# A graph network of four layers: scores of a batch as one product and one sum, and the next-block step moved from behind the passes to their heads

## The reference, cut to what matters

```python
# second layer
Q = node_feats[src] @ W_q + b_q
K = node_feats[dest] @ W_k + b_k
bias = edge_feats @ W_e + b_e
pre = Q + K + bias
act = jnp.where(pre >= 0, pre, SLOPE * pre)
scores = act @ a_w + a_b
...
# last layer
q = x[dst] @ Wq_w + Wq_bias
key_base = x_src @ Wk1 + rel_emb @ Wk2 + Wk_bias
score_base = jnp.einsum('eo,eo->e', q, key_base)
```

## Time and profile before

| what | value |
|---|---|
| median of 3 runs | 8316.85 us (8298.67 to 8347.98) |
| the profiled execution | 8297.37 us, its span 8295.3 us |
| granted TensorE clock over the span | 0.738 |
| busy over the span | PE 63%, DVE 56%, ACT 50%, POOL 60% |

### The profile page before, as it was taken

How to read it: one execution, slowest core, us unless ns; L and a number is a source line. 1 busy time by engine, 2 the same in 40 slices (tenths; PEclk the granted TensorE clock), 3 DMA queues, 4 the chain that set the end, 5 groups by cost and what they waited for, 6 DMA issues and landing times. The chain is left out here.

```text
span 8295.3 us, 160086 instructions
## 1 busy us (share of the span) xinstructions
PE 5185.0 (63%) x37998; PEld 3831.1 (46%) x38194; DVE 4646.3 (56%) x21263; ACT 4171.3 (50%) x11643; POOL 4948.9 (60%) x5713
## 2 busy tenths in 40 slices
PE   4666666666664444445445449996666666666664
PEld 3556555655552222222222228884444444444443
DVE  5555555555545454455445459996555555555556
ACT  3555555555524343344344349993555555555554
POOL 5555555555536556556556539993566666666663
PEclk7888888888876666666666669997666666666666
DMA  3333333333334444455444438884222222222221
GB/s 113 90 89 88 90 88 90 88 90 89 89 91 135 132 134 132 133 134 138 132 132 135 129 99 269 268 267 175 64 63 64 64 64 64 64 63 65 63 64 42
DMA packets 673100, 908.82 MB, mean 110 GB/s; under 512 B 141463, under 2 KB 430217, under 8 KB 672730
## 3 DMA queue, kind: packets, MB, share of 16 engines
q1 hardware_dynamic: 502654, 605.53, 23.3%
q0 software_dynamic: 168944, 301.30, 15.1%
q10 hardware_dynamic: 1357, 0.47, 0.0%
HBM read 696.57 MB, written 210.28 MB: 109 GB/s over the span
## 5 line engine op out<-in xcount | busy, mean ns | idle before, releaser
L801 POOL DMA_INDIRECT rows<-src_rows,idx_slots x1531 | 1469.1, 960 | 1007.9 <-issue 485.3
L801 POOL DMA_INDIRECT rows<-rel_rows,idx_slots x1531 | 1451.3, 948 | 967.3 <-remote 397.0
L801 POOL DMA_INDIRECT rows<-node_rows,idx_slots x1339 | 1279.3, 955 | 928.6 <-remote 338.6
L1399 ACT ACTIVATE onehot<-ident,fresh_slots 128x128 f32<-128x128 f32 x3136 | 993.0, 387 | 1501.5 <-remote 1079.1
L1390 PE MATMUL bank<-onehot,ones 128*128 128x512 f32 x1568 | 1317.0, 937 | 215.5 <-issue 129.8
L1097 ACT ACTIVATE dst_pairs<-pre,minus_node 128x512 bf16<-128x512 int16 x816 | 581.1, 718 | 1091.9 <-remote 589.5
L1488 PE MATMUL bank<-w_e,edge_in 128*128 128x256 f32 x784 | 405.8, 616 | 1045.7 <-remote 504.9
L1127 PE MATMUL bank<-by_chunk,dst_pairs 128*128 128x192 bf16 x6144 | 775.9, 270 | 301.8 <-issue 232.8
L1488 PEld LDWEIGHTS bank<-w_e,edge_in 128*128 128x128 f32 x784 | 210.5, 300 | 1438.3 <-issue 1103.9
L1127 PEld LDWEIGHTS bank<-by_chunk,dst_pairs 128*128 128x128 bf16 x6144 | 585.4, 108 | 381.0 <-issue 281.8
L1127 PE MATMUL bank<-wide_room,dst_pairs 128*128 128x192 bf16 x3264 | 477.6, 278 | 452.1 <-ACT dst_pairs L1101 255.6
(11 more groups left out here) (309 smaller groups left out, 11923.4 us busy)
## 6 DMA issues: line engine op xcount, KB each, us to landing
edge_in<-dst_line SPq DMA_DIRECT2D x392, 256.0 KB
spill<-rows SPq DMA_DIRECT2D x392, 256.0 KB
rows<-spill SPq DMA_DIRECT2D x392, 256.0 KB, 3.1
hot_rows<-rows SPq DMA_DIRECT2D x98, 712.0 KB
onehots<-hot_rows SPq DMA_DIRECT2D x196, 356.0 KB, 3.5
onehots<-src_low SPq DMA_DIRECT2D x98, 512.0 KB
edge_in<-in_ea_l SPq DMA_DIRECT2D x98, 256.0 KB
edge_in<-in_eaT_l SPq DMA_DIRECT2D x392, 64.0 KB
```

The source lines that it names most:

```text
L801: pool.indirect_dma_start(out=to[:, b.slot(ROW_RING), g, :], out_offset=None, in_=table, in_offset=bass.IndirectOffsetOnAxis(ap=idx[:, col ...
L1399: last = act.activation(diag[:, b.slot(2), g, :], ident[:, :], ACT.Copy, scale=fresh_slots[:, b.slot(2 * RING), g:g + 1])
```

## The change: what it does

In both attention layers the stage `scores` becomes two stages. `product` multiplies all 4 tiles in one instruction of 256 elements a partition, and `scores` adds them up, with one `reduce_sum` that writes all 4 scores. In the score sweep `product` stands behind `tops`, and `scores` where it stood; in the attention sweep `product` stands where `scores` stood, and `scores` behind `take`.

The phases behind the sweeps go. Their steps are done by DVE at the head of each sweep instead (`next_window`), and so that the first window comes out right, the places are set one window back before a sweep (`+ WINDOW` for `dst_rel`, `- WINDOW` for `base` and `window_lane`). The copies of `dst_pairs` in the resets go, as the head step writes it. PE waits for the new `base` before its loop in the two attention sweeps.

```diff
-            with nc.Fori(0, windows):
-                sweep()
-                with Phase(nc, name + "_next") as ph:
-                    s = ph.sem("set")
...
+        def next_window(dve, s_stepped, s_based, steps):
+
+            c = Chain(dve, s_stepped)
+            for step in steps:
+                step(dve, c)
+            dve.tensor_scalar(base[:, :], base[:, :], WINDOW, LAST_BASE, ALU.add,
+                              ALU.min).then_inc(s_based, 1)
+            dve.wait_ge(s_based, 1)
...
-        n_reset = 5
+        n_reset = 3
...
-                pool.tensor_copy(to, of).then_inc(s_set, 1)
+                pool.tensor_single_scalar(to, of, by, ALU.add).then_inc(s_set, 1)
...
 # score_sweep
-                            for g in range(TILES_PER_BATCH):
-                                last = dve.tensor_tensor_reduce(
-                                    out=product_out[:, g, :], in0=looked(b)[:, g, :],
-                                    in1=a_w[:, :], scale=1.0, scalar=0.0, op0=ALU.mult,
-                                    op1=ALU.add, accum_out=fresh_slots[:, b.slot(2 * RING), g:g + 1])
-                            last.then_inc(s_score, 1)
+                            dve.tensor_tensor(product_out, looked(b), a_w[:, :].unsqueeze(1)
+                                              .to_broadcast([P, TILES_PER_BATCH, D]), ALU.mult)\
+                               .then_inc(s_product, 1)
+
+                        def scores(b):
+                            done(dve, s_product, b)
+                            dve.reduce_sum(fresh_slots[:, b.slot(2 * RING), :], product_out, AX)\
+                               .then_inc(s_score, 1)
...
                         pipeline(dve, [(9, maxima), (4, join), (11, sums), (9, running), (4, leak),
-                                       (9, tops), (0, hot), (9, biases), (4, scores)])
+                                       (9, tops), (4, product), (0, hot), (9, biases), (4, scores)])
...
 # attention_sweep
+                            dve.tensor_tensor(pre[:, 0, :, :], looked(b),
+                                              rows[:, b.slot(ROW_RING), :, 0:D], ALU.mult)\
+                               .then_inc(s_product, 1)
...
+                            dve.reduce_sum(fresh_slots[:, b.slot(2 * RING), :], pre[:, 0, :, :], AX)\
+                               .then_inc(s_score, 1)
...
-                                       (1, scores), (3, take), (3, differ), (5, add), (0, build),
+                                       (1, product), (3, take), (1, scores), (3, differ), (5, add), (0, build),
```

More of the change, by code:

```diff
@@ L895, in far_stage @@
             return fars
-        n_reset = 5
+        n_reset = 3
         def reset_windows(pool, s_set):
[L901 to L905, removed]
-                pool.tensor_copy(to, of).then_inc(s_set, 1)
+            for n, (to, of, by) in enumerate(((dst_rel[:, :], dst_rel0[:, :], float(WINDOW)),
+                                              (window_lane[:, :], lane[:, :], float(-WINDOW)),
+                                              (base[:, :], base0[:, :], -WINDOW))):
+                pool.tensor_single_scalar(to, of, by, ALU.add).then_inc(s_set, 1)
                 pool.wait_ge(s_set, n + 1)
@@ L1226, in _ @@
                                  unroll=GATHER_UNROLL)
-            windows_loop(name, sweep, [next_places])
+            windows_loop(sweep)
         def kept_sum_sweep(name):
@@ L1520, in leak, with product @@
                                .then_inc(s_act, 1)
-                        def scores(b):
+                        def product(b):
                             done(dve, s_act, b)
@@ L1710, in scores @@
                                 dve.wait_ge(s_score, b.v)
-                            for g in range(TILES_PER_BATCH):
-                                last = dve.tensor_tensor_reduce(
-                                    out=pre[:, 0, g, :], in0=looked(b)[:, g, :],
-                                    in1=rows[:, b.slot(ROW_RING), g, 0:D], scale=1.0,
-                                    scalar=0.0, op0=ALU.mult, op1=ALU.add,
-                                    accum_out=fresh_slots[:, b.slot(2 * RING), g:g + 1])
-                            last.then_inc(s_score, 1)
+                            dve.tensor_tensor(pre[:, 0, :, :], looked(b),
+                                              rows[:, b.slot(ROW_RING), :, 0:D], ALU.mult)\
+                               .then_inc(s_product, 1)
+                        def scores(b):
+                            done(dve, s_product, b)
+                            dve.reduce_sum(fresh_slots[:, b.slot(2 * RING), :], pre[:, 0, :, :], AX)\
+                               .then_inc(s_score, 1)
                         def maxima(b):
@@ L2005, in _ @@
                 act.activation(max_by_chunk[:, :], max_by_chunk[:, :], ACT.Exp).then_inc(s_exp, 1)
-                act.activation(dst_rel[:, :], dst_rel0[:, :], ACT.Copy).then_inc(s_places, 1)
-                for t in range(2):
-                    act.activation(dst_pairs[:, :, t], dst_rel0[:, :], ACT.Copy)\
-                       .then_inc(s_places, 1)
+                act.activation(dst_rel[:, :], dst_rel0[:, :], ACT.Copy, scale=1.0,
+                               bias=float(WINDOW)).then_inc(s_places, 1)
                 act.wait_ge(s_joined, BLOCKS)
```

40 lines of the change are left out of this document (22 added, 18 removed).

## The result

The changed kernel takes 8379.63 us (median of 7 runs, 8371.43 to 8390.56) against 8314.22 us (8298.67 to 8347.98): ratio 1.0071, 95% interval 1.0056 to 1.0086. It is 0.7% slower; I had forecast 8231 us, with a range that ended at 8365 us.

What follows compares the result with a forecast made beforehand. No engine is full; a cadence of gathers and POOL's pauses bounds the two attention sweeps. -73 (score sweep) + 0 (attention sweep) - 14 + 1 = -86 us gives 8231 us; own range 8190 to 8285, with rivals 8090 to 8365.

Steps and rivals of the forecast that it cites:

- The score sweep, -73 us: Score sweep: fewer DVE instructions bring 1.602 down to 1.554 us a gather, 73 us less; bounds no gain and 216 us.
- slow regime: Second half of a run of gathers: each DVE instruction costs a turn of about 1.3 us, so their number counts.
- signs that I had named: Score sweep: gathers towards 1.55 us, fewer unexplained DVE idle times, pause under 2.5 us or after 12 gathers, not 8.
- That pace must be near that of the attention sweep: Score sweep: with DVE's instructions no longer awaited by POOL, it takes the attention sweep's pace, 1.554 us a gather.
- The prices in the free regime: DVE where an instruction costs its work: product 0.34 us plus sum 0.31 us, 0.65 against 0.58 us a batch.
- The sum behind `take`, 0 us: Attention sweep: sum between `take` and `differ` adds 0.19 us a batch, costed at nothing as DVE's wait covers it.
- Rival C: Attention sweep: the sum's 0.19 us is kept in every batch, +74 us, +27 in the score sweep; 8405 us, chance 0.17.
- The step moved, -13 us: Sweep ends and heads: phases behind the sweeps go, 14 us less (10 to 19), with 1 us back at the heads.
- B: Score sweep: the turns only move, pace stays 1.602 us a gather; 8304 us, chance 0.26 together with another rival.
- A: Score sweep: POOL no longer pauses after every 8 gathers, 216 us less, 13 for the steps; 8088 us, chance 0.15.

Runs made afterwards that it cites:

- e2: Against the kernel before: step moved to the sweep heads and new product-and-sum form in the score sweep only, attention sweep with four fused instructions; ratio 1.0054.
- e1: Against the kernel before: only the step moved to the sweep heads, both sweeps keep the four fused score instructions; ratio 0.9974.
- e5: e1 with one more DVE product of 256 elements, read by nothing, ahead of the score sweep's four fused instructions; ratio 0.9959 to the kernel before.
- e4: e2 with the score sweep's product at the end of the step, directly ahead of the sum; ratio 1.0037 to the kernel before.
- g4: e3 with two idle POOL products behind each batch's gathers in the score sweep, the second of 64 elements; ratio 0.9874 to the kernel before.
- f3: The changed kernel with two idle POOL products behind each batch's gathers in the score sweep; ratio 0.9896 to the kernel before.
- e3: Against the kernel before: step moved to the sweep heads and new form in the attention sweep only, score sweep with four fused instructions; ratio 0.9956.
- f1: The changed kernel with one idle POOL product behind each batch's gathers in the score sweep; ratio 1.0035 to the kernel before.
- g1: e2 with six useless one-element-a-partition DVE copies behind the sum in the score sweep; ratio 0.9981 to the kernel before.
- h1: g4 with the same idle POOL products in the attention sweep too; ratio 0.9812 to the kernel before, 8140 us beside 8297.

## Why the prediction was wrong

- **The score sweep, -73 us.** This step failed, and it is the whole error but for small terms that nearly cancel: it measured +83 us in the two profiles and +66 us between e2 and e1, so it was 156 or 139 us off, where the forecast as a whole was 149 us off. It rested on "The lower bound is no gain, as the turns are only moved": that fewer instructions can't hurt. They did, with DVE's own work 0.08 us longer a batch and that increase harmless (e5 adds 0.34 us for nothing). The sentence ahead of it had the mechanism: "where DVE gets to `join` sooner, POOL pauses later". I took a later pause for good. It makes the row of gathers 12 long, the slow regime falls on PE's small matmuls more often (their waits for nothing went from 127 to 311), and once in 8 batches (as e4 shows it) a pause of 5 to 6 us follows. Two of the signs that I had named for the gain came true beside the loss: the pause after 12 gathers and not 8, and fewer unexplained idle times on DVE before the scores (33 us and not 288). Neither is a sign of time.
- **That pace must be near that of the attention sweep**, 1.554, was a neighbour's number, with no run that tied it to this sweep. The sweep can run at 1.57 to 1.58 (g4, f3), but by evening out POOL, not by easing DVE.
- **The prices in the free regime** held: the product 0.33 us from start to start (3583.25 to 3583.58 in the trace of after) where I had 0.34, the sum also 0.33 (3584.12 to 3584.45) where I had 0.31, its duration 409 ns for an estimate of 385. The sum, too, lets the next instruction start before its own end. The Trainium skill, VectorE: DVE Perf Modes, The DRAIN you can't avoid, adds to the rule that I weighed that an instruction which isn't held starts earlier; I had left this out, and the rows fit it.
- **The sum behind `take`, 0 us.** It held. From `take` to `differ` it is 0.45 us in the rows below, where I had 0.39 and before had 0.20, and the sweep didn't feel it: e3 is not slower than e1. Rival C ended on the right side for a wrong reason, its place was the attention sweep. The cover that I counted on is still there: DVE's idle time before `take` is 436 us between 5900 and 8040 us, 461 before the change. In the changed kernel `take`, sum and `differ` stand as forecast, and are over (7008.98) long before POOL's next pause ends (7013.57):

```profile
7008.38 0.16 DVE L1782 TENSOR_REDUCE below_max<-bank 128x4 f32<-128x12 f32 x1
7008.49 0.42 DVE L1727 TENSOR_REDUCE fresh_slots<-pre 128x4 f32<-128x256 f32 x1
7008.83 0.15 DVE L1788 TENSOR_TENSOR below_max<-fresh_slots,below_max 128x4 f32<-128x4 f32 x1
```

- **The step moved, -13 us.** Right, inside the interval: 22 us (11 to 32) in e1; in the profile 5.6 us between the first two sweeps, 1.2 between the score and the attention sweep and 4.5 behind the last. The same tail as the earlier trace rows has no step, and DVE goes from the last sum straight on:

```profile
8308.64 0.28 DVE L1804 SCALAR_TENSOR_TENSOR wide_room<-wide_room,shrink,bank 128x65 f32 x1 [2.29 <-PE bank L1705]
8310.78 0.14 DVE L2210 MEMSET by_chunk<- 64x100 f32 x1 [1.86 <-PEq L230]
```

- **The rivals.** C was nearest in number (8405 us), by a path that wasn't taken; B (the turns only move) was nearest in mechanism, but allowed no loss; A fell wholly. Missing was: *the changed rhythm of DVE locks POOL into a worse pattern*. The earlier trace rows would have let me ask for it: the slow regime is bound to the second half of a run of 8, so a run of 12 has it over 8 gathers and not over 4.

Not settled: what the slow regime is. It takes the semaphore and register instructions of DVE and SP, PE's weight loads and DVE's accumulator reads alike, but not ACT's register and semaphore instructions. On DVE it comes from about the fifth gather of a run on, and goes with a rest of 0.93 us (g4) but not of 0.63 us (f1). It comes in that form only in the score sweep, whose rows are of 768 bytes and which also writes them out again; I didn't try which of these it needs. Nor is it shown why fewer and longer instructions on DVE make POOL's runs longer: that they do is shown (g1, e2), the way from one to the other is only argued.

## What to carry to other kernels

When a producer runs ahead in bursts and the consumers stall inside each burst, the consumer's rhythm can set the burst's length, and fewer instructions on it can make it worse: count the run lengths and the pauses before pricing instructions, and give "less work" a lower bound under zero. Here the cure was at the producer. The kernel with idle POOL products of about 0.9 us behind each batch's gathers in both attention sweeps (h1) is 1.9% faster than the one before. Of that, 0.4% is what the moved step and the attention sweep's new form bring (e3); the idle products bring the rest, more than anything done to the scores.

## What the runs showed of the hardware

In the score sweep gathers of 128 rows start 1.25 us apart. From about the fifth of a run on, with no wait on record, DVE's instructions start up to 1.3 us apart and more, and weight loads of PE up to 1.3 and 2.0 us apart (e4). Register and semaphore instructions that take 0.6 to 1.5 us instead of 0.02 to 0.1: in the changed kernel 441 on DVE, 498 on SP, 4 on PE, none on ACT; with a rest of 1.3 us behind every fourth gather (f3) none on DVE, 77 on SP, 17 on PE, none on ACT. Reductions of 256 elements to 4 took 409 to 414 ns, and the next instruction began 0.33 to 0.34 us after their start.
